# Performer block and expert block in one program on one Trainium2 core: another order of the batch loop, key sums without added constants

## The chip, the cores and the metric

One Trainium2 core runs the whole program in one launch. The metric is the device time of one execution in microseconds (us), lower is better. The time given for a kernel is the median of its runs. Engines: PE (TensorE; PEld is its weight load), DVE (VectorE), ACT (ScalarE), POOL (GpSimd), SP (SyncE, which issues most DMAs).

## The reference, cut to what matters

All tensors are float32. The input is 8 batches of 512 tokens of 256 values.

```python
# attention half, once per batch b (16 heads of 16 values, 64 random features)
a  = layernorm(x)                                 # no gain
q, k, v = a@Wq.T+bq, a@Wk.T+bk, a@Wv.T+bv         # split into heads
xp = einsum('bhnd,md->bhnm', t*16**-.25, proj)    # features of q and of k
qp = exp(xp_q - diag_q - max over m   ) + 1e-4
kp = exp(xp_k - diag_k - max over n, m) + 1e-4
out = (qp @ (kp.T @ v)) / (qp @ sum_n kp)         # heads
r  = a + out@Wo.T + bo
x2 = layernorm(r)*g2+be2
z  = layernorm(x2 + relu(x2@W1.T+b1)@W2.T+b2)*g3+be3
x1 = x + layernorm(z)
# expert half, over all 4096 tokens
xf = layernorm(x1); scores = softmax(xf@gate.T); each of 8 experts takes its top 512 tokens,
adds its two-layer MLP of them, weighted by the score; result = x1 + layernorm(that)
```

## The kernel before, in words

**Layout.** 128 partitions; a batch is TT = 4 tiles of 128 tokens. The 8 pairs of heads (PAIRS) make the 1024 columns of the key features `kp` ([128, 4, 1024]) and query features. The four PSUM banks `pX` hold features, `pA` (2 banks) the attention products, `pF` (2 banks) the feed-forward products, each used in turn: a product waits until the copy of the one before it in its bank is done.

**Stages.** A prologue, a software-pipelined loop over the 8 batches (until about 466 us), a tail that ends batch 7, the choice of the experts' tokens (about 510 to 566 us), eight experts, the last layer norm. Only the loop, the batch 0 ahead of it and SP's outputs are touched here.

**The batch loop.** `batches` calls `body(i, f, u)` on every engine: attention of batch i, feed-forward of batch f = i-1, gates and outputs of batch u = i-2, for i = 0 to 7. Bodies 3 to 6 are one hardware loop; 0, 1, 2 and 7 stand by themselves (`is_first`, `is_ahead`, `is_last`). There is no planner: each engine works off its own list in the order in which the code stands, and waits on semaphores. So the order of calls in the four `body` functions is the schedule.

**PE's list in one body.** Keys and queries (24 products of float32r, `by_halves`), values, turning x2, `key_features(0)`, turning the keys, `hidden(0)` to `hidden(7)` (six matmuls each, W1) with `key_features(1)`, `features` of the queries (two halves), `turn_kmax` and `spread_kmax` in between, then 32 products with W2 (`ff_out`, two instructions each) that are cut up to stand between `turn_tops`, `features_turned(0)`, `context`, `features_turned(1)`, `sums_of_keys`, `turn_context`, `all_heads`, `gates`, `turn_x`; `attention_out` (Wo, 24 matmuls) is last. `features` and `features_turned` run in tiles of 32 rows, `context`, `sums_of_keys`, `all_heads` and `gates` in tiles of 32 columns, all others on the full array.

**The key path.** `xk_copy` (ACT) takes the features out of PSUM; `k_max` (DVE) takes maxima; `turn_kmax`, `k_top` (`smax`, `sdiag`), `spread_kmax` make one stabilizer per head; `k_shift` and `k_sub` (DVE) subtract it; `exp_k` and then `eps_k` (ACT) give exp and exp + 1e-4; POOL adds the four token tiles into `ksum` (line 1055, three operations); `context` multiplies with v. In batch 0 there is no `eps_k`: an additional matmul with a constant adds it, and DVE does the sums.

**The query path.** `q_max` (DVE) takes maxima of the query features from PSUM, `parts_of_tops` splits them into two parts (line 1296 a cast, line 1298 a subtraction, both within SBUF), `turn_tops` (PE) turns them, `q_tops` (ACT) copies them, `features_turned` makes the shifted features anew, `exp_q` (ACT) their exp.

**The end of a body.** `all_heads` gives denominators, which `dens` (ACT) copies, and heads; `heads_out` (DVE) divides: a reciprocal (line 1313) and a product; the two groups of heads follow each other, with the gates' copy `turned_gates` (DVE) between them. `heads_top` (ACT) and `rest_of_heads` (DVE) split the result for `attention_out`.

**Layer norms.** `stats` (DVE), `root` and `shift` (POOL), `normed` (DVE) or `z_norm`, `x_norm`, `xf_norm` (ACT). `z_affine`, the two operations on x2, and `xnb` (line 1049) are POOL operations of a whole batch. `residual` (DVE, line 1336) adds x and z, both in SBUF.

Of the kernel before, what the change touches and what calls it, by code (L numbers as in the profile page):

```python
# [6 lines left out]
ALU = mybir.AluOpType  # L7
# [23 lines left out]
N_CONST = 11  # L31
# [83 lines left out]
def build(nc, video, WqT, bq, WkT, bk, WvT, bv, WoT, bo, projT, W1T, b1, W2T, b2, g2, be2, g3, be3,  # L115
          gateT, ln_w, ln_b, fc1T, b1s, fc2T, b2s, out):
    with ExitStack() as ctx:
# [39 lines left out]
        epsk_c = sb("epsk_c", [P, 1])  # L157
        eps4_c = sb("eps4_c", [P, 1])
# [3 lines left out]
        ksum = sq[:].rearrange("p a b d -> p (a b d)")  # L162
        dgk = sb("dgk", [P, TT, H])
# [14 lines left out]
        sdiag = sb("sdiag", [H, H])  # L178
        ones_h = sb("ones_h", [H, P])
        kbias = sb("kbias", [P, TT, H])  # L180
        kp = sb("kp", [P, TT, H * M])
# [13 lines left out]
        vsum = cs[:].rearrange("p n x -> p (n x)")  # L195
# [26 lines left out]
        kp_f, qe_f, qp_f = (a[:].rearrange("p a b -> p (a b)") for a in (kp, qe, qp))  # L222
# [110 lines left out]
        ksum_ready, ks_ready, ke_ready, kp_ready = sem("ksum_ready"), sem("ks_ready"), sem("ke_ready"), sem("kp_ready")  # L333
# [112 lines left out]
        def _(sp):  # L446
# [11 lines left out]
            def outputs(u):  # L458

                wait(sp, x1_out, 16 * u)  # L460
                wait(sp, xf_ready, u)
                sp.dma_start(x1[:], vid_d[u]).then_inc(xres_in, 16)

                for ready, done, dst, src in ((x1_ready, x1_out, out_t[u], x1[:]), (xf_ready, xf_out, acc_t[u], xf[:]),
                                              (y_ready, y_out, row_t[u][:, :, 0:D], y[:]),
                                              (sc_ready, sc_out, row_t[u][:, :, D:ROW], sct[:])):
                    sp.wait_ge(ready, u + 1)
                    sp.dma_start(dst, src).then_inc(done, 16)

# [35 lines left out]
            load_expert(0)  # L505
            for ready, done, dst, src in ((x1_ready, x1_out, out_t[L1], x1_end[:]), (sc_ready, sc_out, row_t[L1][:, :, D:ROW], sct[:]),
# [29 lines left out]
        def _(act):  # L536
# [40 lines left out]
            def xk_copy(i, t):  # L577

                act.wait_ge(x_ready, i * X_JOBS + J_XK + t // 2 + 1)
                nc.scalar.activation(kp[:, t, :].rearrange("p (a b) -> p a b", a=4), features_of(t), ACT.Copy).then_inc(xk_ready, 1)  # L580
# [14 lines left out]
            def cs_copy(i, n):  # L595
                act.wait_ge(a_ready, i * A_JOBS + J_CTX + n + 1)
                nc.scalar.activation(cs[:, n, :], pA[n][:, 0:G * P], ACT.Copy).then_inc(cs_ready, 1)

            def exp_k(i, t):

                act.wait_ge(ks_ready, i * TT + t + 1)
                nc.scalar.activation(kp[:, t, :], kp[:, t, :], ACT.Exp).then_inc(kp_ready if is_first(i) else ke_ready, 1)

            def eps_k(i, t):
                act.wait_ge(ke_ready, (i - 1) * TT + t + 1)
                nc.scalar.activation(kp[:, t, :], kp[:, t, :], ACT.Identity, bias=epsk_c[:, 0:1]).then_inc(kp_ready, 1)  # L606
# [91 lines left out]
            def body(i, f, u):  # L698
# [17 lines left out]
                elif att:  # L716
                    keys(i)
                    queries(i, 0)
                    queries(i, 1)
                    values(i, 0)  # L720
                    values(i, 1)
                if ff:
                    for c in range(C):
                        take_f(f, J_X2T + c, x2T_hi[:, c, :], ACT.Copy, x2T_ready)
                if is_ahead(i):
                    key_rows(1)
                elif att:
                    key_rows(0)
                    squares(i, 0)
                    squares(i, 1)  # L730
                if ff:
                    relu(f, 0)
                    relu(f, 1)
                if att and not is_ahead(i):
                    key_rows(1)
                if ff:
                    relu(f, 2)
                    relu(f, 3)
                if att:
                    q_squares(i)  # L740
                if ff:
                    for n in range(4, FC):
                        relu(f, n)
                        if ut and n < FC - 1:
                            z_norm(u, n - 4)
                        if ut and n == FC - 2:
                            z_norm(u, 3)
                if att:
                    for t in range(2):
                        exp_k(i, t)  # L750
                        eps_k(i, t)
                    q_tops(i)
                    for t in range(2, TT):
                        exp_k(i, t)
                        eps_k(i, t)
                    exp_q(i, 0)
                    cs_copy(i, 0)
                    exp_q(i, 1)
                    cs_copy(i, 1)
                if ut:  # L760
                    xf_norm(u)
                if att:
                    dens(i)
# [9 lines left out]
                if att:  # L773
                    x_norm(i + 1)
                if ut:
                    normed_rows(u)
                if att:
                    heads_top(i, 0)
                    heads_top(i, 1)
                    xT_copy(i + 1)  # L780
                if ut:
                    exp_logits(u)

# [132 lines left out]
        def _(pool):  # L916
# [8 lines left out]
            nc.gpsimd.memset(epsk_c[:], EPS_K).then_inc(const_ready, 1)  # L925
            nc.gpsimd.memset(eps4_c[:], N // P * EPS_K).then_inc(const_ready, 1)
            nc.gpsimd.memset(mxp, 0.0).then_inc(const_ready, 1)
            nc.gpsimd.memset(ones_h[:], 1.0).then_inc(const_ready, 1)

# [83 lines left out]
            def body(i, f, u):  # L1013
# [10 lines left out]
                if f is not None:  # L1024

                    pool.wait_ge(f_ready, f * F_JOBS + J_X2T + 2)
                    nc.gpsimd.tensor_tensor(x2[:], x2[:], g2_b[:].unsqueeze(1).to_broadcast([P, TT, D]), ALU.mult).then_inc(x2b_ready, 1)
                if u is not None:
                    root(3, u)
                    shift(3, u, nz)  # L1030
                if f is not None:
                    pool.wait_ge(x2b_ready, 2 * f + 1)
                    nc.gpsimd.tensor_tensor(x2[:], x2[:], b2_b[:].unsqueeze(1).to_broadcast([P, TT, D]), ALU.add).then_inc(x2b_ready, 1)
                if is_first(i):
                    root(0, 1)
                    shift(0, 1, nx)

                    pool.wait_ge(v_ready, 2)
                    halves = v.rearrange("p (k a) d -> p k (a d)", k=2)
                    nc.gpsimd.tensor_tensor(vsum[:], halves[:, 0], halves[:, 1], ALU.add).then_inc(vsum_ready, 1)  # L1040
                    pool.wait_ge(vsum_ready, 1)
                    nc.gpsimd.tensor_tensor(vsum[:, 0:D], vsum[:, 0:D], vsum[:, D:2 * D], ALU.add).then_inc(vsum_ready, 1)
                if i is not None:

                    if isinstance(i, int) and i == 0:
                        pool.wait_ge(bias_ready, 1)
# [4 lines left out]
                    for t in range(1, 1 if is_first(i) else TT):  # L1051
# [3 lines left out]
                        nc.gpsimd.tensor_tensor(ksum, kp[:, 0, :] if t == 1 else ksum, kp[:, t, :], ALU.add).then_inc(ksum_ready, 1)  # L1055
# [141 lines left out]
        def _(dve):  # L1197
# [36 lines left out]
            def k_max(i, t):  # L1234

                dve.wait_ge(xk_ready, i * TT + t + 1)
                nc.vector.tensor_reduce(mxk[:, t, :], kp[:, t, :].rearrange("p (h m) -> p h m", m=M), AX_X,
# [15 lines left out]
            def k_top(i, steps):  # L1253
# [3 lines left out]
                nc.vector.tensor_scalar(sdiag[:], ident[0:H, 0:H], smax[:, 0:1], None, ALU.mult).then_inc(stab_ready, 1)  # L1257
# [1438 lines left out]
```

## Time and profile before

| | us |
|---|---|
| median of 3 runs (787.88 to 789.0) | 787.96 |
| the profiled execution's own time | 789.41 |
| its span (first to last instruction) | 787.7 |
| PE busy, share of the span | 724.5, 92% |
| PEld busy | 592.8, 75% |
| DVE busy | 619.9, 79% |
| ACT busy | 469.8, 60% |
| POOL busy | 377.1, 48% |

Busy times are sums over the span. PE's matmuls overlap in the pipeline and their ends are modelled, so the start of one and the start of the next tell what it costs. The mean granted PE clock was 0.967 of full speed. The loop's part is the stretch to 466 us.

### The profile page before, as it was taken

What the parts mean: (1) busy time and instruction counts of PE and PEld (TensorE: products, weight loads), DVE (VectorE), ACT (ScalarE), POOL (GpSimd) and SP (SyncE); (2) the same over time, 40 slices, a digit from 0 to 9 for tenths busy, and PEclk for the clock granted to TensorE, in tenths of its full rate; (3) what the DMA queues carried; (4) which work ended last, traced back from release to release, by engine and by line L of the source; (5) the groups of instructions that cost most, each with busy time, mean ns of one, the idle gap of its engine ahead of it and who ended that gap; (6) DMA issues with size and microseconds to landing.
All of it is one profiled execution on the core that took longest, in us unless ns stands there. A gap on an engine that the chain in (4) does not pass through costs nothing. (4 is left out here: it accounts for less than half of the span.)

```text
span 787.7 us, 16101 instructions
## 1 busy us (share of the span) xinstructions
PE 724.5 (92%) x5948; PEld 592.8 (75%) x5948; DVE 619.9 (79%) x1307; ACT 469.8 (60%) x749; POOL 377.1 (48%) x358
## 2 busy tenths in 40 slices
PE   8999999999999999999999979875899999999950
PEld 7867768778778778778678668765788889998850
DVE  5876678888888888888898797888857777677683
ACT  4656747867867767868857835464245544455470
POOL 4364317527527527617616613511437576554563
PEclk9899999999999999999999999999699999999985
DMA  8100010011011011011011021250346664456593
GB/s 250 34 2 2 1 54 2 27 54 57 28 53 54 27 53 54 27 53 54 27 54 30 32 71 35 62 190 1 93 161 170 154 158 105 115 152 167 130 270 115
DMA packets 51184, 62.60 MB, mean 79 GB/s; under 512 B 9408, under 2 KB 44992, under 8 KB 51136
## 3 DMA queue, kind: packets, MB, share of 16 engines
q1 hardware_dynamic: 44016, 49.74, 19.5%
q0 software_dynamic: 6864, 12.19, 7.9%
q8 instruction: 30, 0.49, 0.3%
q14 instruction: 18, 0.15, 0.1%
q10 hardware_dynamic: 256, 0.03, 0.0%
HBM read 40.85 MB, written 21.10 MB: 79 GB/s over the span
## 5 line engine op out<-in xcount | busy, mean ns | idle before, releaser
L2166 PE MATMUL pF<-w,h 128*128 128x256 f32 x448 | 109.8, 386 | 0.0
L2166 PEld LDWEIGHTS pF<-w,h 128*128 128x128 f32 x448 | 80.7, 190 | 17.6 <-issue 8.6
L1131 POOL DMA_INDIRECT kp<-row_scratch,idx_g x32 | 43.2, 1350 | 73.5 <-DVE idx_g L1838 49.7
L896 ACT ACTIVATE h<-pX,b1cur 128x512 f32<-128x512 f32 x64 | 44.0, 689 | 53.8 <-DVE b1cur L1938 39.4
L2618 PE MATMUL pX<-w_lo,h_hi 128*128 128x256 f32 x256 | 73.9, 289 | 0.8 <-issue 0.8
L985 POOL TENSOR_SCALAR ve<-mv 128x4 f32<-128x4 f32 x36 | 8.5, 236 | 134.4 <-DVE mv L1208 133.4
L2618 PE MATMUL pX<-w_hi,h_lo 128*128 128x256 f32 x256 | 72.4, 283 | 0.0
L2618 PE MATMUL pX<-w_hi,h_hi 128*128 128x256 f32 x256 | 72.4, 283 | 0.0
L1139 POOL DMA_INDIRECT acc_scratch<-qp,idx_s x28 | 58.0, 2073 | 22.3 <-DVE qp L1875 17.4
L1896 DVE TENSOR_TENSOR h_lo<-h,h_hi 128x512 fp32r<-128x512 f32 x64 | 42.7, 690 | 24.6 <-ACT h_hi L888 24.6
L1313 DVE RECIPROCAL den<-den 128x512 f32<-128x512 f32 x14 | 46.9, 3348 | 7.9 <-ACT den L544 7.9
L1055 POOL TENSOR_TENSOR sq<-kp 128x1024 f32<-128x1024 f32 x7 | 23.3, 3333 | 61.7 <-ACT kp L606 61.7
L549 ACT ACTIVATE h<-pF,b1c 128x512 f32<-128x512 f32 x56 | 38.7, 691 | 20.6 <-PE pF L2103 20.6
L2103 PE MATMUL pX<-x2T_hi,w_lo 128*128 128x512 f32 x128 | 50.7, 396 | 0.0
L2103 PE MATMUL pX<-x2T_lo,w_hi 128*128 128x512 f32 x128 | 50.6, 395 | 0.0
L2103 PE MATMUL pX<-x2T_hi,w_hi 128*128 128x512 f32 x128 | 50.6, 395 | 0.0
L2618 PEld LDWEIGHTS pX<-w_lo,h_hi 128*128 128x128 f32 x256 | 49.0, 191 | 1.8 <-issue 1.0
L2618 PEld LDWEIGHTS pX<-w_hi,h_lo 128*128 128x128 f32 x256 | 49.0, 191 | 0.1
L2618 PEld LDWEIGHTS pX<-w_hi,h_hi 128*128 128x128 f32 x256 | 49.0, 191 | 0.0
L2103 PE MATMUL pF<-x2T_hi,w_lo 128*128 128x512 f32 x112 | 47.6, 425 | 0.5 <-DVE x2T_lo L1440 0.5
L2103 PE MATMUL pF<-x2T_hi,w_hi 128*128 128x512 f32 x112 | 44.3, 396 | 0.0
L2103 PE MATMUL pF<-x2T_lo,w_hi 128*128 128x512 f32 x112 | 44.2, 395 | 0.0
(434 smaller groups left out, 2157.9 us busy)
## 6 DMA issues: line engine op xcount, KB each, us to landing
kp<-fc1T SPq DMA_DIRECT2D x8, 1024.0 KB, 7.2
w<-fc2T SPq DMA_DIRECT2D x8, 1024.0 KB, 8.2
xin<-video SPq DMA_DIRECT2D x7, 512.0 KB, 3.7
x<-video SPq DMA_DIRECT2D x7, 512.0 KB, 4.4
out<-x SPq DMA_DIRECT2D x7, 512.0 KB, 3.0
acc_scratch<-xf SPq DMA_DIRECT2D x7, 512.0 KB, 2.9
row_scratch<-y SPq DMA_DIRECT2D x7, 512.0 KB, 3.0
kp<-acc_scratch SPq DMA_DIRECT2D x4, 512.0 KB, 5.3
```

The costliest lines, as they stand in the source:

```text
L549: nc.scalar.activation(dst, pF[n % 2][:], func, **kw).then_inc(done, 1)
L896: nc.scalar.activation(h[:, n, :], pM[n % M_SLOTS], ACT.Gelu_apprx_tanh, bias=b1cur[:, n:n + 1]).then_inc(he_ready, 1)
L985: nc.gpsimd.tensor_scalar(ve[k][:], mv[k][:, :, 1], LN_EPS, None, ALU.add).then_inc(ve_ready[k], 1)
L1055: nc.gpsimd.tensor_tensor(ksum, kp[:, 0, :] if t == 1 else ksum, kp[:, t, :], ALU.add).then_inc(ksum_ready, 1)
L1131: pool.indirect_dma_start(xg[:, g, :], None, row_d, bass.IndirectOffsetOnAxis(ap=idx_g[:, g:g + 1], axis=0)).then_inc(gathered, 16)
L1139: pool.indirect_dma_start(acc_d, bass.IndirectOffsetOnAxis(ap=idx_s[:, g:g + 1], axis=0), og[:, g, :], None, compute_op=ALU.add).then_inc( ...
L1313: steps.link(nc.vector.reciprocal(den[:, g, :], den[:, g, :]))
L1896: nc.vector.tensor_tensor(h_lo[:, n, :], h[:, n, :], h_hi[:, n, :].bitcast(F32), ALU.subtract).then_inc(h_lo_ready, 1)
L2103: ins = nc.tensor.matmul(dst[:], w_[:, k, tok(n)], x_[:, k, :], start=(m == 0), stop=(m == len(parts) - 1))
L2166: ins = nc.tensor.matmul(pF[m][:, half * D:(half + 1) * D], h[:, k, tok(2 * m + half)], w2[:, k, :], start=(k == 0), stop=(k == FC - 1))
L2618: ins = nc.tensor.matmul(pM[2 + m][:, t2 * D:(t2 + 1) * D], h_[:, k, tok(2 * m + t2)], w_[:, k, :], start=(not last and k == 0 and j == 0) ...
```

## The change

What it does:

- **Key tiles are 130 columns wide per pair.** `kp` becomes `kpe` [128, 4, 8 pairs, 130]; columns 128 and 129 hold 1e-4 from the start. `eps_k` is gone in every batch. `context` multiplies v with 129 columns, so column 128 of its result is 1e-4 times the sum of v; `cs_copy(0)` copies that column out and adds it as a bias (one small and two larger ACT operations in place of one); `cs_copy(1)` adds 512e-4 as a bias. In batch 0 the constant matmuls of `context` and `sums_of_keys` and POOL's sums of v are gone.
- **`sdiag` and `ones_h` have 128 rows** (zeros below row 16), so `spread_kmax` runs on the full array.
- **PE:** `key_features(0)` ahead of the values, `key_features(1)` ahead of `hidden(0)`, `hidden` cut differently, `turn_tops`, `context`, `features_turned(0)` next to each other, `sums_of_keys`, `features_turned(1)`, `turn_context` next to each other; W2's 32 products cut into 8, 4, 4, 5, 3, 3, 5.
- **DVE:** z is normed before `scores`; `k_max` 0 and 1 ahead of `x2T_lo`, 2 and 3 ahead of z's second statistics; `k_top` ahead of `q_max` 0 and 1; all four `k_sub` ahead of `q_max` 2 and 3 and `parts_of_tops`; `scores` of the batch before after these; both divisions ahead of `turned_gates`.
- **ACT:** `exp_k` between the last `relu`s, `z_norm` behind `exp_k`, `cs_copy` ahead of `exp_q`, `dens` ahead of `xf_norm`, `normed_rows` last.
- **POOL:** the key sums wait for all four `k_sub` first; `xnb` goes behind all roots; x2's second operation goes ahead of the third root.
- **SP:** the DMA of the scores goes one body later.

```diff
+PW = P + 2
-        kp = sb("kp", [P, TT, H * M])
+        kpe = sb("kp", [P, TT, PAIRS, PW])
+        kp = kpe[:, :, :, 0:P]
...
-                nc.scalar.activation(cs[:, n, :], pA[n][:, 0:G * P], ACT.Copy).then_inc(cs_ready, 1)
+                if n:
+                    nc.scalar.activation(cs[:, 1, :], pA[1][:, 0:G * P], ACT.Identity, bias=epsn_c[:, 0:1]).then_inc(cs_ready, 1)
+                else:
+                    wide = pA[0][:, 0:G * PW].rearrange("p (g x) -> p g x", x=PW)
+                    nc.scalar.activation(vsum[:].unsqueeze(2), wide[:, :, P:P + 1], ACT.Copy).then_inc(vsum_ready, 1)
+                    act.wait_ge(vsum_ready, i + 1)
+                    for g in range(G):
+                        ins = nc.scalar.activation(cs[:, 0, g * P:(g + 1) * P], wide[:, g, 0:P], ACT.Identity, bias=vsum[:, g:g + 1])
+                    ins.then_inc(cs_ready, 1)
...
# POOL
+                if is_first(i):
+                    pool.wait_ge(bias_ready, 1)
+                    biased_rows()
+                else:
+                    pool.wait_ge(ks_ready, (i + 1) * TT)
+                    for t in range(1, TT):
...
+                if not is_first(i):
+                    biased_rows()
...
# DVE, after kmax
                 if u is not None:
                     dve.wait_ge(za_ready, 2 * u + 2)
                     stats(3, su, z)
+                k_top(i, sa)
+                q_max(i, 0)
+                q_max(i, 1)
+                dve.wait_ge(dg_ready, (i + 1) * 2)
+                k_shift(i)
+                k_sub(i, 0)
+                k_sub(i, 1)
+                rest_of_squares(i)
+                k_sub(i, 2)
+                k_sub(i, 3)
+                q_max(i, 2)
+                q_max(i, 3)
+                parts_of_tops(i)
+                if more:
+                    ln1_stats(i + 1)
+                if u is not None and not (isinstance(u, int) and u == 0):
+                    scores(u - 1)
...
-                    heads_out(i, 0, sa)
+                heads_out(i, 0, sa)
+                heads_out(i, 1, sa)
                 if u is not None:
                     turned_gates(u * U_JOBS + J_G)
...
# PE, from key_features(1) on
+                key_features(1)
+                pe.wait_ge(x2l_ready, (f + 1) * C)
...
+                hidden(0)
+                hidden(1)
+                pe.wait_ge(qT_ready, (i + 1) * G)
+                features(i, J_XQ, qT, 0)
+                hidden(2)
+                turn_kmax()
+                hidden(3)
+                hidden(4)
+                spread_kmax()
+                hidden(5)
+                features(i, J_XQ + 1, qT, 1)
+                hidden(6)
+                hidden(7)
+                ff_out(8)
+                turn_tops()
+                context()
+                features_turned(0)
+                ff_out(4)
+                sums_of_keys()
+                features_turned(1)
+                turn_context()
+                ff_out(4)
+                all_heads()
+                ff_out(5)
```

## Rows read from the trace of the kernel before

**Rows 1.** Windows of one loop body: busy per engine (instructions), PE clock, DMA, GB/s.
```profile
260.00:319.00 59.00, 58.93 (x530) 45.19 (x529) 50.84 (x98) 43.76 (x64) 30.10 (x28) 1.00 0.13 45
```

**Rows 2.** Timeline of PE, a loop body: start, us, engine, line, out<-in, [idle before].
```profile
258.91 4.48 PE L2166 MATMUL pF<-w,h 128*128 128x256 f32 x20
263.23 0.60 PE L2073 MATMUL pX<-ident,qe 128*128 128x128 f32 x4
...
268.11 0.70 PE L2166 MATMUL pF<-w,h 128*128 128x256 f32 x2
268.74 1.95 PE L2256 MATMUL pA<-kp,qe 128*32 128x128 f32 x64
...
275.20 1.03 PE L2166 MATMUL pF<-w,h 128*128 128x256 f32 x4
276.20 3.89 PE L2175 MATMUL pA<-qp,cdbd 128*32 128x512 f32 x32
...
285.76 1.46 PE L2166 MATMUL pF<-w,h 128*128 128x256 f32 x6
286.87 0.47 PE L2297 MATMUL pX<-wo_lo,aT_hi 128*128 128x256 f32 x1
...
290.26 0.40 PE L2103 MATMUL pA<-x2T_hi,wk_lo 128*128 128x512 f32 x1
...
295.86 0.40 PE L2093 MATMUL pA<-wv_lo,x2T_hi 128*128 128x256 f32 x2
...
299.64 1.17 PE L2114 MATMUL pX<-projbd,qp 32*128 32x128 f32 x32
300.74 1.09 PE L2073 MATMUL pA<-ident,qp 128*128 128x128 f32 x8
...
312.66 0.27 PE L2182 MATMUL pA<-ident,kmax 128*16 128x128 f32 x1
```

**Rows 3.** Timeline of DVE, the same stretch.
```profile
255.21 0.94 DVE L1257 TENSOR_SCALAR sdiag<-ident,smax 16x16 f32<-16x16 f32 x1
...
257.77 2.36 DVE L1261 TENSOR_TENSOR kp<-kp,kbias 128x1024 f32<-128x1024 f32 x2
260.04 2.35 DVE L1287 TENSOR_REDUCE mxq<-pX 128x16 f32<-128x1024 f32 x2
262.52 0.20 DVE L1296 CAST qe<-mxq 128x64 fp32r<-128x64 f32 x1
262.75 0.23 DVE L1298 TENSOR_TENSOR qe<-mxq,qe 128x64 f32<-128x64 f32 x1
...
265.17 3.38 DVE L1336 TENSOR_TENSOR x<-x,z 128x1024 f32<-128x1024 f32 x1
...
312.97 0.28 DVE L1256 TENSOR_REDUCE smax<-pA 16x1 f32<-16x128 f32 x1 [0.72 <-PE pA L2182]
313.29 0.92 DVE L1257 TENSOR_SCALAR sdiag<-ident,smax 16x16 f32<-16x16 f32 x1
```

**Rows 4.** Timeline of POOL, the same stretch.
```profile
264.13 3.34 POOL L1055 TENSOR_TENSOR sq<-kp 128x1024 f32<-128x1024 f32 x1 [8.01 <-ACT kp L606]
267.55 5.70 POOL L1055 TENSOR_TENSOR sq<-sq,kp 128x1024 f32<-128x1024 f32 x2
...
311.78 2.40 POOL L1049 TENSOR_TENSOR xnb<-xn,bo_b 128x1024 f32<-128x1024 f32 x1
```

**Rows 5.** Timeline of ACT, one addition of the constant.
```profile
260.77 1.15 ACT L606 ACTIVATE kp<-kp,epsk_c 128x1024 f32<-128x1024 f32 x1
```

**Rows 6.** Timeline of DVE in body 1, which has no batch u.
```profile
81.89 0.22 DVE L1257 TENSOR_SCALAR sdiag<-ident,smax 16x16 f32<-16x16 f32 x1
```

**Rows 7.** Timeline of PE in batch 0, in body 1 and in body 7.
```profile
44.83 0.42 PE L2272 MATMUL pA<-eps_c,ones 128*32 128x128 f32 x8
...
113.63 0.50 PE L2297 MATMUL pX<-wo_hi,aT_lo 128*128 128x256 f32 x2 [1.03 <-DVE aT_lo L1277]
...
464.61 0.47 PE L2093 MATMUL pX<-wo_lo,aT_hi 128*128 128x256 f32 x2 [1.49 <-DVE aT_lo L1549]
```

More of the change, by code:

```diff
@@ L719, in body @@
                     queries(i, 1)
+                    key_rows(0)
                     values(i, 0)
                     values(i, 1)
[L722 to L728, printed above, removed]
+                for c in range(C):
+                    take_f(f, J_X2T + c, x2T_hi[:, c, :], ACT.Copy, x2T_ready)
@@ L729, in body @@
+                if not is_ahead(i):
                     squares(i, 0)
                     squares(i, 1)
[L731 to L759, printed above, removed]
+                key_rows(1)
+                relu(f, 0)
+                relu(f, 1)
@@ new lines, in body @@
+                q_squares(i)
+                for n in range(2, 6):
+                    relu(f, n)
+                exp_k(i, 0)
+                relu(f, 6)
+                exp_k(i, 1)
+                relu(f, 7)
+                exp_k(i, 2)
+                exp_k(i, 3)
+                if ut:
+                    z_norm(u, 0)
+                    z_norm(u, 1)
+                q_tops(i)
+                if ut:
+                    z_norm(u, 2)
+                    z_norm(u, 3)
+                cs_copy(i, 0)
@@ L1036, in body, with biased_rows @@
                     shift(0, 1, nx)
[L1038 to L1046, printed above, removed]
+                def biased_rows():
                     wait(pool, r_ready, i * 2)
@@ L2157, in hidden, with ff_out @@
                     by_halves(slot_f(f, J_H + n), w1_hi, w1_lo, x2T_hi, x2T_lo, n).then_inc(f_ready, 1)
-                def ff_out(m, half, k0=0, k1=FC):
-                    if half == 0:
-                        slot_f(f, J_Y + m)
-                    for k in range(k0, k1):
+                products = [(m, half, k) for m in range(2) for half in range(2) for k in range(FC)]
+                def ff_out(count):
+                    for m, half, k in products[:count]:
+                        if half == k == 0:
+                            slot_f(f, J_Y + m)
                         if m == half == 0:
@@ L2167, in ff_out @@
                                                start=(k == 0), stop=(k == FC - 1))
-                    if half == 1 and k1 == FC:
-                        ins.then_inc(f_ready, 1)
+                        if half == 1 and k == FC - 1:
+                            ins.then_inc(f_ready, 1)
+                    del products[:count]
                 def by_heads(j, w_, g):
@@ L2422, in body @@
-                if att:
-                    features(i, J_XQ + 1, qT, 1)
-                    spread_kmax()
-                if ff:
-                    hidden(7)
-                if ff:
-                    ff_out(0, 0)
-                    ff_out(0, 1, 0, 2)
-                if att:
-                    turn_tops()
-                if ff:
-                    ff_out(0, 1, 2, FC)
-                if att:
-                    features_turned(0)
-                if ff:
-                    ff_out(1, 0, 0, 1)
@@ L2438, in body @@
-                if att:
-                    context()
-                    features_turned(1)
-                if ff:
-                    ff_out(1, 0, 1, 3)
-                if att:
-                    sums_of_keys()
-                if ff:
-                    ff_out(1, 0, 3, 4)
-                if att:
-                    turn_context()
-                    if ff:
-                        ff_out(1, 0, 4, 6)
-                if att:
-                    all_heads()
+                key_features(1)
```

211 lines of the change are left out of this document (75 added, 136 removed).

## The prediction

> **What bounds the kernel now.** I read the window table first, since the share of the whole span mixes stages. In a loop body PE is busy 58.93 of 59.00 us at the full clock, the others 50.84 (DVE), 43.76 (ACT) and 30.10 (POOL) [rows 1]. So a body lasts as long as PE's own list, and a faster engine elsewhere buys nothing unless PE waited for it. The same instruction comes again after 58.08 us (`sdiag` at 255.21 and at 313.29 [rows 3]); that is a body. Since the ends of matmuls are modelled, a busy PE can hide small losses, so the second view is PE's timeline, read from start to start [rows 2]. It shows three sorts of loss. (a) The last three products with W2 start at 285.76 and Wo's first matmul at 286.87; Wo's 24 matmuls then take until 290.26, 3.39 us. 24 float32r matmuls of 512 columns take 5.60 (290.26 to 295.86), so 256 columns should take about 2.8. The W2 piece took 1.11 where six instructions at 4.32/20 = 0.216 need 1.30, so 0.19 of the 3.39 is its. The rest, 0.4 us, is a wait for the divided heads. (b) A piece of W2 between tiled work costs more than its instructions: two from 268.11 to 268.74 take 0.63 for 0.43, four from 275.20 to 276.20 take 1.00 for 0.86. That is about 0.1 at each change between the full array and tiles. (c) In bodies 1 and 7 the wait for the heads is open: 1.03, and 1.49 [rows 7].
>
> Third, DVE and POOL in the same stretch, because the new order puts DVE's query maxima under POOL's key sums [rows 3, 4]. DVE's residual of 1024 columns takes 3.38 where `k_sub` of 1024 columns takes 2.36/2. It ended at 268.55, 1.1 after POOL's first sum (264.13 + 3.34 = 267.47); POOL's next two then took 5.70 for what is otherwise 2.35 each, 1.0 more. Likewise `sdiag`, 16 columns, takes 0.92 under POOL's `xnb` (311.78 + 2.40 = 314.18, `sdiag` ends at 314.21), and 0.22 where POOL is idle [rows 6]. So these DVE operations and POOL's exclude each other.
>
> **The change part by part, a loop body.**
>
> *Work removed from ACT.* Four operations of 1.15 [rows 5], 4.6 us, against about 1 us for the cut-up `cs_copy`. ACT had 15 us of slack [rows 1] and PE did not wait for it. Taken as 0; the bounds are -0.4 (if the earlier exp took away a wait) and +0.3. PE's 129th column is 1/128 of the 1.9 us of `context` (268.74), 0.02. `spread_kmax` on the full array changes its surroundings by 0.1 at most, either way: 0.
>
> *Fewer changes of tiling.* Before, the stretch from `turn_tops` to `all_heads` changes between full array and tiles six times; after, `context` stands next to `features_turned(0)` and `sums_of_keys` next to `features_turned(1)`: four. Of the pieces of W2 inside, one is gone and two longer ones remain. At 0.1 a change and 0.1 for what the pieces lost besides: -0.3. Bounds: 0, if going from row tiles to column tiles costs as much as going by way of the full array, and -0.6, if each of the removed four sides was worth 0.15. Beyond that stretch the number of changes is the same.
> The Trainium skill ("TensorEngine Tiling (Array Packing)", Key Properties) says that changing the mode drains the engine, and row tiles and column tiles are two modes. By it the stretch has six changes instead of seven (six and `context` to `features_turned(1)`; now four and two), the term would be -0.1, and the total 1 us less good; my rows have no undisturbed step between the two kinds to test it.
>
> *The wait ahead of Wo.* Between the first of `all_heads` (276.20) and Wo stand 10 products of W2 before and 16 after (5+3+3+5), 6 x 0.43 = 2.6 us more cover for the divisions; and the second division no longer stands behind the gates' copy. The 0.4 goes: -0.4. What is late next is whatever must be ready 2.6 + 0.3 us earlier: the key and query path ahead of `all_heads`.
>
> *That path.* I walked it from `turn_kmax` to `turn_tops`. PE after: five `hidden` of 1.40 (5.60/4) = 7.0, one half of the features 1.10 (299.64 to 300.74), 8 products of 0.43 = 3.46, and `spread_kmax` with its surroundings about 0.5: `turn_tops` is wanted 12.1 after `turn_kmax`. DVE after: `turn_kmax` to `sdiag` 313.29 - 312.66 = 0.63, `sdiag` 0.22 (`xnb` no longer runs then), `q_max` 2.3, `k_shift` 0.3, `k_sub` 2.27 (257.77 to 260.04), the squares' rest 1.2 (of the size of a `k_sub`), `k_sub` 2.27, `q_max` and its gap 2.48 (260.04 to 262.52), cast and subtraction 0.46: 12.1. So the tops arrive just as PE wants them, with no margin: 0 taken, +0.7 if `sdiag` is still held up, and more in the rival below. POOL's sums start after the last `k_sub`, at about 9.2 in the same count, and end 3 x 2.43 later at 16.5; PE wants them after `turn_tops` 0.4, `context` 1.9, `features_turned(0)` (at least the 1.1 of a half of the features) and four products 1.7, at 17.2 or later. They are in time. SP's score DMA and `scores`, one body later, stand ahead of nothing that PE waits for.
>
> *Sum of a body:* -0.3 - 0.4 + 0.1 for small misfits = -0.6, five bodies (2 to 6): -3.0.
>
> **The other bodies.** Batch 0: 16 constant matmuls go (8 instructions are 0.22 to 0.42 [rows 7]), in a stretch that runs as a chain; `cs_copy(0)` gets 0.5 longer beside it. -0.7, bounds -1.0 and +0.5. Body 1: -0.3 for tiling, the wait of 1.03 and the rest of its kind, together -1.4, go; but both `k_max` now stand ahead of `x2T_lo`, where one did, and PE's `hidden(0)` waits for that: +1.2 (half of `q_max`'s 2.35, the same size); and +0.3 for tops without margin. -0.2. Body 7: its end is the chain of DVE's half divisions from `all_heads` to Wo's second half [rows 7], so it moves by the whole amount by which `all_heads` moves: 2.6 + 0.3 = -2.9. Behind it the tail is a chain, too, and nothing takes that back.
>
> Total: -3.0 - 0.7 - 0.2 - 2.9 = -6.8 us on an execution of 789.4 (span 787.7, 1.7 around it). The median of 3 is 1.45 below that execution; I carry the difference over: 787.96 - 6.8 = **781.2**.
>
> **Rivals.**
>
> *1. The subtraction of the tops waits for POOL's second sum (slower).* POOL's first sum now starts with the end of the last `k_sub`, lasts 2.36 and is followed 0.08 later by the second (267.47, 267.55 [rows 4]): that asks for the ports 2.5 after `k_sub`'s end. `q_max` starts 0.09 before that end (260.13, 260.04), the subtraction (line 1298) 2.71 after `q_max`: at 2.6. Behind POOL by 0.1, it waits for the whole second sum and PE's `turn_tops` with it: 2.4 us a body, against a gain of 0.6. It decides at 0.1 us; a POOL operation of 8 x 130 columns or one more wait ahead of it may well be that much slower, and the free-standing bodies have smaller gaps on DVE than the loop. In the four bodies of the hardware loop alone: -6.8 + 4 x 2.4 = +2.8, **790.8**. In all seven: +10, **798**.
> The Trainium skill ("SBUF — State Buffer", Who interferes with whom) states this rule: a VectorE instruction with two SBUF inputs and a GpSimd instruction that reads SBUF exclude each other for the whole instruction, and the first to issue wins. By that rule, the cast ahead of it may also take both ports. The trace agrees for the residual (3.38 for 1.2) and for `sdiag`.
>
> *2. `sdiag` is still held up,* now by the third root, which POOL starts at about the same time. For: it starts right after z's statistics, which now stand ahead of `k_top`. Against: a root works on 4 columns. Price 0.7 in each of six bodies: -6.8 + 4.2 = -2.6, **785.4**.
>
> *3. The order gains nothing in the loop:* tiling changes cost the same in any neighbourhood, a wait of 0.4 appears at another hand-over (`all_heads` for the second exp of the queries, or `turn_x`, both within 0.3 us by the same walk), and body 7 keeps a part. About -1, **787**.
>
> **How the numbers follow.** Forecast 0.46, its own range 779.0 to 784.0. Rival 1 in the loop alone 0.20, in all bodies 0.12; rival 2 0.12; rival 3 0.10. The range of 8 in 10 leaves out rival 1 in all bodies and a little below: 779.0 to 791.5. What a measurement can tell from no change is 0.2%, 1.6 us. Faster: forecast and rival 2, 0.58. Same: rival 3, 0.10. Slower: 0.32.
>
> **What would show it.** Right: `sdiag` at 0.22 us; PE's body 57.5; Wo from its first matmul to the next keys 2.8 to 3.0; the subtraction of the tops (line 1298 before) at 0.2; body 7's last wait for the heads still there, but 2.9 earlier. Rival 1: the subtraction at 2.2 to 2.6 us, PE idle ahead of `turn_tops` by as much, a body of 59.9. Rival 2: `sdiag` at 0.9, PE idle 0.7 ahead of `turn_tops`. The forecast is wrong in its base if PE waits by more than 0.3 anywhere else in bodies 2 to 6.

## The result, and the profile after

| | before | after |
|---|---|---|
| median of the runs, us | 787.91 (787.55 to 789.0, 5 runs) | 792.64 (788.32 to 798.94, 5 runs) |
| profiled execution / its span, us | 789.41 / 787.7 | 798.94 / 797.2 |
| busy PE, DVE, ACT, POOL, us (after) | | 726.3, 621.6, 443.1, 359.0 |

The ratio is 1.0055 (95% interval 1.003 to 1.008): a loss of 4.7 us against a forecast of -6.8. The second thing to see is the spread: 1.5 us before, 10.6 after. The profiled execution is the slowest of the five, so it shows the loss at its largest.

The quickest way to place a loss in a program that repeats is a list of starts of one instruction. I took the first matmul of `turn_tops` in each batch (PE's timeline) and subtracted:

| kernel | batch 0 to 1 | 1 to 2 | 2 to 3 | 3 to 4 | 4 to 5 | 5 to 6 | 6 to 7 | 7 to the turn of x2 | behind it |
|---|---|---|---|---|---|---|---|---|---|
| before | 52.53 | 57.29 | 57.97 | 58.07 | 58.08 | 58.07 | 58.08 | 28.73 | 321.5 |
| after | 51.62 | 55.80 | 59.50 | 62.03 | 62.09 | 59.42 | 57.50 | 29.27 | 322.0 |
| `e1_guard` (below) | 51.39 | 55.79 | 57.46 | 57.45 | 57.40 | 57.40 | 57.49 | 29.32 | 321.9 |

One thing in this table is bookkeeping: the change puts 16 matmuls with W2 ahead of the tops where 20 stood, so from body 1 on the tops come 4 x 0.23 = 0.9 us earlier within a body. That 0.9 shows as a gain in the first period and is missing again behind the tops of batch 7.

The loss sits in four bodies, 3 to 6, which are the passes of the hardware loop. There PE stands still ahead of the turned tops. PE in body 4 (timeline: start, us, engine, line, out<-in, idle before and its releaser):

```profile
263.74 1.24 PE L2159 MATMUL pF<-w,h 128*128 128x256 f32 x5
266.90 0.94 PE L2064 MATMUL pX<-ident,qe 128*128 128x128 f32 x4 [1.92 <-DVE qe L1300]
267.77 3.30 PE L2247 MATMUL pA<-kp,qe 128*32 128x129 f32 x64
271.00 1.14 PE L2202 MATMUL pX<-qT,projbd 32*128 32x512 f32 x8
...
282.23 1.92 PE L2169 MATMUL pA<-qp,cdbd 128*32 128x512 f32 x16 [0.96 <-ACT den L554]
```

The releaser is the subtraction of the tops. DVE and then POOL in the same stretch; they answer to [rows 3, 4]:

```profile
261.90 2.35 DVE L1289 TENSOR_REDUCE mxq<-pX 128x16 f32<-128x1024 f32 x2
264.38 0.20 DVE L1298 CAST qe<-mxq 128x64 fp32r<-128x64 f32 x1
264.61 2.24 DVE L1300 TENSOR_TENSOR qe<-mxq,qe 128x64 f32<-128x64 f32 x1
...
279.05 2.14 DVE L1307 TENSOR_TENSOR csum_own<-csum,epsmask 128x8 f32<-128x8 f32 x1
```
```profile
262.15 2.37 POOL L1054 TENSOR_TENSOR sq<-kp 128x1024 f32<-128x1024 f32 x1 [7.16 <-DVE kp L1263]
264.60 4.42 POOL L1054 TENSOR_TENSOR sq<-sq,kp 128x1024 f32<-128x1024 f32 x2
...
278.79 2.37 POOL L1043 TENSOR_TENSOR xnb<-xn,bo_b 128x1024 f32<-128x1024 f32 x1
```

POOL's second key sum starts at 264.60, DVE's subtraction at 264.61; the subtraction, 0.22 us of work, takes 2.24 and ends when POOL's second sum does (4.42 is the time of the second and the third together). In all four loop bodies POOL is ahead by 0.01 us or level; in bodies 1 and 2 the subtraction starts 0.06 before (89.20 and 89.26, 145.00 and 145.06) and takes 0.22. The same thing happens once more at 279.05: POOL's `xnb`, 0.26 us ahead, holds an 8-column product for 2.14; the bias that `dens` (ACT) waits for comes from that product, and the last two head products wait 0.96 for ACT's copies.

A third price comes from PE's clock (windows: us, then PE, PEld, DVE, ACT, POOL busy, granted clock, DMA, GB/s). First body 4, its stop and the 4.2 us behind it, then the same in body 5:

```profile
264.90:266.90 2.00, 0.08 (x1) 0.00 (x1) 2.00 (x2) 0.34 (x1) 1.92 (x2) 1.00 0.00 0
266.90:271.10 4.20, 4.20 (x72) 3.39 (x72) 3.76 (x15) 1.58 (x3) 2.12 (x1) 0.59 0.00 0
```
```profile
327.00:328.90 1.90, 0.06 (x1) 0.00 (x0) 1.90 (x2) 0.32 (x1) 1.85 (x1) 1.00 0.00 0
329.00:331.40 2.40, 2.40 (x68) 2.10 (x68) 2.00 (x11) 1.57 (x3) 2.12 (x1) 1.00 0.00 0
```

After 1.92 us without work the granted clock was 0.59 on average in body 4, between its levels of 1.2 and 2.4 GHz, and the turned tops with `context` took 4.10 us; after the same stop in body 5 it stayed at 1.00 and they took 2.48 (328.99 to 331.47). So a body that loses takes 2.0 more, and in two of the four 2.6 on top, 1.6 of it the clock and 1.0 the wait at 282.23.

The stop ahead of body 3's tops was followed by a slow stretch too (0.60 over 204.87 to 209.00), the one ahead of body 6's was not.

What the forecast named for the loop body itself is there. PE and DVE, bodies 5 and 6, answering to [rows 2, 3]:

```profile
353.01 0.47 PE L2285 MATMUL pX<-wo_lo,aT_hi 128*128 128x256 f32 x1
...
356.00 0.39 PE L2094 MATMUL pA<-x2T_hi,wk_lo 128*128 128x512 f32 x1
```
```profile
374.86 0.22 DVE L1258 TENSOR_SCALAR sdiag<-ident,smax 16x16 f32<-16x16 f32 x1
```

Wo takes 2.99 us instead of 3.39, `sdiag` 0.22 instead of 0.92. In the last batch, DVE's copy of the gates and PE's two waits ahead of Wo, answering to [rows 7]:

```profile
465.85 0.29 DVE L1345 COPY gT<-pF 128x128 f32<-128x128 f32 x1 [2.66 <-PE pF L2130]
```
```profile
465.13 0.65 PE L2130 MATMUL pF<-qe,gate 128*32 128x128 f32 x16
...
469.06 0.47 PE L2084 MATMUL pX<-wo_lo,aT_hi 128*128 128x256 f32 x2 [1.79 <-DVE aT_lo L1540]
...
473.60 0.48 PE L2084 MATMUL pX<-wo_lo,aT_hi 128*128 128x256 f32 x2 [0.62 <-DVE aT_lo L1540]
```

### The profile page after: what moved, and what is told of

It reads as the page before. It is cut to its first block and busy times, and to the rows that moved or that the text cites. A ratio compares the mean times of both kernels' runs of the same rounds, so it can differ in the third digit from the quotient of the medians.

```text
span 797.2 us, 16016 instructions
## 1 busy us (share of the span) xinstructions
PE 726.3 (91%) x5916; PEld 597.3 (75%) x5916; DVE 621.6 (78%) x1307; ACT 443.1 (56%) x737; POOL 359.0 (45%) x357
## 5 line engine op out<-in xcount | busy, mean ns | idle before, releaser
L2159 PE MATMUL pF<-w,h 128*128 128x256 f32 x448 | 106.5, 384 | 0.0
L1238 DVE TENSOR_REDUCE mxk<-kp 128x16 f32<-128x1024 f32 x32 | 37.5, 1213 | 6.9 <-ACT kp L590 6.9
```

The costliest lines, as they stand in the source:

```text
L1238: nc.vector.tensor_reduce(mxk[:, t, :].rearrange("p (s h) -> p s h", h=2), kp[:, t].rearrange("p s (h m) -> p s h m", m=M), AX_X, ALU.max) ...
L2159: ins = nc.tensor.matmul(pF[m][:, half * D:(half + 1) * D], h[:, k, tok(2 * m + half)], w2[:, k, :], start=(k == 0), stop=(k == FC - 1))
```

## The experiments

Each was timed in 4 to 12 runs against runs of the kernel before on the same chip. The main theory: in the loop the subtraction of the tops and POOL's second key sum are in a dead heat, and a lost one costs a body 2 us or more. The rivals: the new order of PE's work or the 129th column costs the time; the spread is only the granted clock's. Different experiments ran on different chips, so a comparison between two of them rests on the ratios to the kernel before, or on the traces.

**`e1_guard`.** POOL's second sum also waits for the tops' two parts.

```
                         if t > 1:
                             pool.wait_ge(ksum_ready, i * (TT - 1) + t - 1)
+                        if t == 2:
+                            pool.wait_ge(qmx_ready, (i + 1) * TOPS)
```

> The changed kernel, and POOL's second key sum also waits until the tops' two parts are stored. Theory (a dead heat between the subtraction of the tops and that sum): the subtraction takes 0.22 us in all 8 batches, PE goes from W2 to the turned tops without a wait, and the five runs lie within 1.5 us of one another. From the changed kernel's profiled 798.9 go 4 stalls of 1.93 and 1.8 of slow PE behind one of them: about 789.4, so 787 to 790. Rival (the loss is in the new order of PE's work, or in the 129th column): 791 to 794, as the changed kernel. Rival (the spread is the granted clock's own): the runs still spread over 5 us or more.

Measured: 784.56 us (784.39 to 785.75), ratio 0.9947 (0.9932 to 0.9963). The subtraction takes 0.22 in all 8 batches and the row of the table above has no body over 57.5. DVE, then POOL, in body 4:

```profile
259.06 0.23 DVE L1302 TENSOR_TENSOR qe<-mxq,qe 128x64 f32<-128x64 f32 x1
```
```profile
259.36 4.50 POOL L1056 TENSOR_TENSOR sq<-sq,kp 128x1024 f32<-128x1024 f32 x2 [0.39 <-DVE qe L1302]
```

The time is 2.4 us below the expected range, which had counted four stops and one slow stretch, and neither the second slow stretch nor the waits at the head products. The first rival falls: the same PE order with the same 129 columns is now 4.2 us faster than before. The spread goes from 10.6 us to 1.4, but a spread alone proves no race: the kernel before, on another chip, came to 786.62 to 792.83 us at granted clocks of 0.971 to 0.958. What speaks against the clock as the only cause is two runs of the changed kernel at the same granted clock, 0.967, that took 788.32 and 792.64. The 14.4 us between the two profiled spans are almost all in four periods: 2.0 + 4.6 + 4.7 + 2.0 = 13.3.

**`e2_late` and `e8_lost`.** Can the race be made always lost?

```
                 nc.vector.tensor_copy(hi.bitcast(F32R), whole).then_inc(qmx_ready, 1)
+                nc.vector.memset(spare[:], 0.0)
```

> The changed kernel, and a memset of 64 columns on DVE between the cast and the subtraction of the tops, so that POOL's second key sum is always first. Dead heat theory: the subtraction takes 2.0 to 2.2 us in each of the 7 bodies instead of in some, PE waits some 2 us ahead of the turned tops in each, and the time is the guarded kernel's plus 7 x 2.0 = 14 us or a little more (803 to 806), with a small spread between runs. If the subtraction's start has nothing to do with it, the extra 0.1 us a body gives 793 to 794.

Measured: 787.7 us; five of the six runs lie between 783.66 and 793.58, one at 795.43. Neither expectation holds, and the edit was weaker than meant: the name belonged to a scratch of one column. DVE and POOL in the profiled execution:

```profile
258.19 0.20 DVE L1299 CAST qe<-mxq 128x64 fp32r<-128x64 f32 x1
258.33 0.06 DVE L1300 MEMSET spare<- 128x1 f32 x1
258.41 0.23 DVE L1302 TENSOR_TENSOR qe<-mxq,qe 128x64 f32<-128x64 f32 x1
```
```profile
258.41 4.54 POOL L1055 TENSOR_TENSOR sq<-sq,kp 128x1024 f32<-128x1024 f32 x2
```

The 0.06 us fell into the gap behind the cast, so the subtraction started 0.22 after the cast, as without it. In bodies 3 to 6 POOL's sum started 0.01 ahead of it or level, just as in the changed kernel's profiled execution, and yet DVE won all four here and lost all four there: starts that are equal to 0.01 us don't tell who wins. Another run of the same kernel on the same chip came to 793.58 at the granted clock of this one (0.967 and 0.966), 10 us apart. I take the difference for lost races; only the fast execution was profiled, so this isn't shown. With 512 columns (0.48 us) the edit does what was meant:

> The changed kernel, and a memset of 512 columns (0.2 us or more) on DVE between the cast and the subtraction of the tops. With the memset of 0.06 us POOL and DVE still started within 0.01 us of each other and DVE won each time. Theory (the one that is ready first by more than that holds the other out): the subtraction is held for 1.9 to 2.2 us in bodies 1 to 7, each body is 59.4 to 62.1 long instead of 57.4, and the time is 798 to 806 with a spread of a few us from the granted clock. Rival (not the order but something else decides, and a later subtraction shares the port): 785 to 788.

Measured: 795.83 us (793.41 to 802.06), ratio 1.0094 (1.0057 to 1.013); periods 59.46, 62.04, 62.03, 59.45 in the loop. PE and the windows behind two of the stops:

```profile
268.32 0.91 PE L2066 MATMUL pX<-ident,qe 128*128 128x128 f32 x4 [1.92 <-DVE qe L1302]
283.64 1.92 PE L2171 MATMUL pA<-qp,cdbd 128*32 128x512 f32 x16 [0.94 <-ACT den L555]
```
```profile
268.40:270.40 2.00, 2.00 (x28) 1.58 (x32) 1.81 (x10) 1.14 (x3) 2.00 (x1) 0.55 0.00 0
...
330.40:332.40 2.00, 2.00 (x59) 1.83 (x63) 1.82 (x10) 1.36 (x3) 2.00 (x1) 1.00 0.00 0
```

The theory holds for the loop and its price; it was wrong that bodies 1, 2 and 7 would lose too, and the median lies below the expected 798 to 806. In 1 and 2 the memset started 0.04 to 0.05 ahead of POOL's sum, in the loop 0.03 to 0.04 behind it; in 7 POOL waits 0.44 of its own. In those three bodies the subtraction took 0.15 us although POOL's sum had started 0.36, 0.36 and 0.07 before it, and POOL's pair of sums took up to 4.89 instead of 4.54. So it seems that the memset kept POOL out until the subtraction had started; no run isolates that. The runs still spread over 8.6 us: where the profiled execution lost all four, the price of a lost race is 2.0 or 4.6, so a spread doesn't count the races either.

**`e10_nudge`.** The opposite push: POOL 0.3 later, no wait added.

```
                         if t > 1:
                             pool.wait_ge(ksum_ready, i * (TT - 1) + t - 1)
+                        if t == 2:
+                            settled(pool)
+                            nc.gpsimd.tensor_scalar(nudge_c[:], mhalf[:], LN_EPS, None, ALU.add)
```

(`settled` is one semaphore increment, no wait.)

> The changed kernel, and POOL does one operation of 4 columns (0.2 us) between its first and second key sum; no wait is added. Theory (whoever is ready first holds the other out, and a few hundredths of a us decide): POOL's second sum comes 0.3 us later, DVE's subtraction takes 0.22 in all bodies, 784 to 786 with a spread under 2.5 us. Rival (only an order kept by a wait cures it, since the two engines' times vary between runs): 786 to 794, spread over 4 us.

Measured: 783.02 us (781.29 to 784.17), ratio 0.993 (0.9915 to 0.9946), a little below what was expected, the spread 2.9 instead of under 2.5. DVE and POOL in body 4:

```profile
258.00 0.20 DVE L1302 CAST qe<-mxq 128x64 fp32r<-128x64 f32 x1
258.23 0.23 DVE L1304 TENSOR_TENSOR qe<-mxq,qe 128x64 f32<-128x64 f32 x1
```
```profile
258.34 0.23 POOL L1057 TENSOR_SCALAR nudge_c<-mhalf 128x4 f32<-128x4 f32 x1 [0.20 <-POOL sq L1058]
258.53 4.51 POOL L1058 TENSOR_TENSOR sq<-sq,kp 128x1024 f32<-128x1024 f32 x2
```

0.3 us of distance are as good as a wait: the periods from 2 to 7 are 57.33 to 57.43.

**`e11_cover`.** Is the price PE's standstill, or something behind it on DVE or POOL? (`e8_lost`, with `ff_out(12)`, `ff_out(2)`, `ff_out(2)` in place of 8, 4, 4.)

> The kernel in which POOL is always first in the loop (memset of 512 columns), and 4 of the 8 W2 products that lie behind the turned tops (in two groups) are moved ahead of them: 0.93 us of work while PE waits. Theory (the price of the lost race is PE's idle time, and the granted clock falls after it): PE's idle ahead of the tops goes from 1.92 to about 1.0, some of it comes back as waits of 0.2 to 0.6 further on, and a body in which the clock stays up takes 58.8 to 59.4; where the clock does not fall any more the 2.6 us bodies go too: 790 to 796. Rival (the price lies in DVE's or POOL's later work, not PE's idle): as without this edit, 795 to 796.

Measured: 793.12 us (792.39 to 794.96), ratio 1.0071 (1.0055 to 1.0087). A product is two matmuls of 0.23, so I had counted half: 1.86 us of work moved. PE in body 4:

```profile
264.50 0.66 PE L2066 MATMUL pX<-ident,qe 128*128 128x128 f32 x4 [0.21 <-DVE qe L1302]
270.79 1.14 PE L2204 MATMUL pX<-qT,projbd 32*128 32x512 f32 x8 [0.33 <-ACT qp L639]
274.61 3.80 PE L2171 MATMUL pA<-qp,cdbd 128*32 128x512 f32 x32 [0.53 <-ACT qp L639]
```

The subtraction is still held (1.82), but PE idles 0.21, the clock stays at 1.00 (read behind the tops of bodies 3, 4 and 5), and no body takes 62: the four of the loop take 58.7 each. `csum_own` is not held either (0.17). So the 4.6 us bodies were PE's standstill and what it drew after it. It is no cure: the work that now covers the tops is missing behind them, at two waits for the queries' exp.

**`e3_xnb`.** The guard, and POOL's bias sum behind DVE's reduction (`pool.wait_ge(obias_ready, i + 1)` ahead of `biased_rows()`).

> The guarded kernel, and POOL adds the bias to the normed rows only once DVE has reduced the context's sums. Theory: the product of 8 columns ahead of that reduction takes 0.17 us in all batches instead of up to 2.1, PE's wait ahead of the four head products (1.0 in two bodies, a part of 1 in the last) goes: 1.5 to 2 us less than the guarded kernel, 786 to 788. Rival (ACT's norm of the next rows waits for the later bias sum, or the held product was covered): within 0.5 us of the guarded kernel.

Measured: 786.58 us (784.48 to 787.03), 2.0 above `e1_guard`. `csum_own` takes 0.17 everywhere, and the loop bodies take 57.41: the rival holds. There was nothing to gain in the bodies, since with the guard alone the product took 0.17 in them already; it was held in batch 0 (0.97) and batch 7 (1.43) only. The 2.0 lie elsewhere: 0.98 in the first period, 1.5 behind batch 7, in code that is the same. The granted clock was 0.964 in five of its six runs, 0.967 to 0.969 in those of `e1_guard`, and its one run at 0.967 took 784.48, as `e1_guard` does. I take it for the clock's; the next run, which keeps the edit, bears this out.

**`e4_tail`.** The last one, and in the last batch the copy one place later.

```
             end_heads(1, 0)
-            turned_gates((L2 - 1) * U_JOBS + J_G)
             end_heads(0, 1)
+            turned_gates((L2 - 1) * U_JOBS + J_G)
             end_rest_of_heads(0)
```

> The kernel before this one, and in the last batch DVE copies the gates behind the fourth half head instead of ahead of it. Theory: the copy waited 2.66 us for gates that PE issues 16 matmuls later than it did, and Wo waited 1.79 and 0.62 behind it: 2.0 to 2.4 us less, 784 to 786. Rival (the chain of four half divisions sets the end of that batch whatever the copy does): within 0.5 us of the kernel without this edit.

Measured: 781.89 us (781.01 to 784.27). From the tops to the turn of x2 27.01 us instead of 29.18: -2.2, as expected. The median fell by 4.7, 2.5 more than the edit explains, to below the expected 784 to 786: the first period is back at 51.41 us and the stretch behind the turn takes 320.5 instead of 323.3, the granted clock in its first 7.3 us 1.00 instead of 0.78. That is what `e3_xnb` had lost, and POOL's wait is still in place. DVE and PE, against the rows of the last batch above:

```profile
451.52 0.29 DVE L1348 COPY gT<-pF 128x128 f32<-128x128 f32 x1 [0.48 <-PE pF L2133]
```
```profile
452.59 0.58 PE L2087 MATMUL pX<-wo_lo,aT_hi 128*128 128x256 f32 x2
...
457.09 0.47 PE L2087 MATMUL pX<-wo_lo,aT_hi 128*128 128x256 f32 x2 [0.48 <-DVE aT_lo L1543]
```

**`e7_gates_mid`.** On `e4_tail`, the copy between the two divisions again, in the bodies.

> The kernel with guard, bias sum and tail edits, but DVE copies the gates between the two divisions again, as before the change; PE's gates stay where the change put them. Theory (the tail's loss is a copy that waits for gates issued later): the second division starts at the end of PE's gates, some 2.8 us later in every body, and Wo or the stage behind it waits 1 to 2.5 us of that: 5 to 14 us more in all. Rival (there is slack on DVE behind the divisions): within 0.5 us.

Measured: 783.93 us (782.5 to 784.84) on one chip, `e4_tail` 781.89 on another (ratios 0.9942 and 0.9917). The traces are clearer: 57.84 a body instead of 57.41. DVE and PE in body 5:

```profile
337.14 0.29 DVE L1348 COPY gT<-pF 128x128 f32<-128x128 f32 x1 [2.87 <-PE pF L2133]
```
```profile
341.36 0.47 PE L2288 MATMUL pX<-wo_lo,aT_hi 128*128 128x256 f32 x1
...
344.75 0.40 PE L2097 MATMUL pA<-x2T_hi,wk_lo 128*128 128x512 f32 x1
```

The copy waits 2.87 as expected, but only 0.4 reaches PE: Wo takes 3.39 instead of 3.00. DVE's slack hid the rest, so both expectations missed; and 3.39 is what Wo took before [rows 2]. The divisions side by side are what took that wait away.

**`e6_split`.** On `e4_tail`, W2's products between the tiled groups again.

```
                 turn_tops()
+                ff_out(3)
                 context()
                 features_turned(0)
-                ff_out(4)
+                ff_out(1)
                 sums_of_keys()
+                ff_out(1)
                 features_turned(1)
+                ff_out(1)
                 turn_context()
-                ff_out(4)
+                ff_out(2)
                 all_heads()
```

> The kernel with guard, bias sum and tail edits, but W2's products are again put between the groups that use PE in tiles (tops, 3 products, context, features, 1, key sums, 1, features, 1, turned context, 2, heads); the number of products ahead of the heads and behind them is unchanged. Theory (what a body gained by standing the tiled groups side by side is about 0.3 us): the body goes from 57.4 to 57.6 to 57.8, 1.5 to 2.8 us in all. Rival (the order of PE's groups gains nothing and the 0.65 us a body came from the copy of the gates and Wo's cover alone): within 0.5 us.

Measured: 786.35 us (784.58 to 788.38); 58.0 a body. From tops to heads it takes 11.41 us, `e4_tail` 10.83. `e6_split`, then `e4_tail`:

```profile
382.21 0.70 PE L2162 MATMUL pF<-w,h 128*128 128x256 f32 x2
382.84 0.64 PE L2262 MATMUL pA<-sq,ones 128*32 128x128 f32 x16
383.42 0.70 PE L2162 MATMUL pF<-w,h 128*128 128x256 f32 x2
384.26 1.14 PE L2205 MATMUL pX<-qT,projbd 32*128 32x512 f32 x8
```
```profile
378.43 1.99 PE L2162 MATMUL pF<-w,h 128*128 128x256 f32 x8
380.35 0.65 PE L2262 MATMUL pA<-sq,ones 128*32 128x128 f32 x16
380.92 1.14 PE L2205 MATMUL pX<-qT,projbd 32*128 32x512 f32 x8
```

Two matmuls between tiled groups take 0.63 and 0.84 for 0.46; eight take 1.92 for 1.86. Of the 0.58, two small waits belong to this order and not to the tiling: 383.42 + 0.70 leaves 0.14 ahead of the features (ACT's exp of the queries ends there), and the heads wait 0.13 for the masked context. That leaves 0.3, by subtraction. So the gain of standing the tiled groups side by side is 0.3 us in this comparison, which still mixes several changes of neighbour. The total, 3.6 us by spans (4.5 by medians from two chips), is more than I expected, since I had left those waits out.

**`e5_body1`, `e9_best`, `e12_all`.** On `e4_tail`, in body 1 only, `k_max(i, 1)` behind the low parts of x2T (`e5_body1`); that without the later bias sum (`e9_best`); and with `e10_nudge`'s operation in place of the guard (`e12_all`).

> The kernel with guard, bias sum and tail edits, and in body 1 (whose keys are ready ahead) DVE takes the second key maximum behind the low parts of x2T instead of ahead of them. Theory: PE's wait of 1.25 us ahead of the first hidden product of body 1 goes, so 0.8 to 1.2 less than the kernel without this edit. Rival (the key maxima then end later and the turn of kmax waits): 0 to +0.5.

Measured: 781.65 us (780.01 to 782.22). The period from batch 0 to 1 is 50.60 instead of 51.41, and the wait is down from 1.25 to 0.47:

```profile
69.77 0.50 PE L2100 MATMUL pF<-x2T_hi,w_lo 128*128 128x512 f32 x1 [0.47 <-DVE x2T_lo L1442]
```

> The changed kernel with guard, tail and body 1 edits, without the later bias sum. Theory (that sum lay beside the path: bodies of 57.4 us with it and without it, and the 2 us between the two medians were the granted clock's): within 0.7 us of the kernel with all four, 781 to 782.5. Rival (the bias sum's wait cost the 2 us): 779 to 780.5.

Measured: 782.39 us (780.1 to 784.21): 0.7 above `e5_body1`, which ran on another chip (ratios 0.9926 and 0.9909). The rival (the bias sum's wait costs 2 us) wanted it 1 to 2 us below, and falls.

> The kernel with later bias sum, tail and body 1 edits, and POOL's 4-column operation in place of the guard's wait. From the traces: bodies of 57.33 instead of 57.42 us (6 of them: 0.5 less), the rest as in the kernel with all four edits: 780 to 782, spread under 4 us. If the small operation loses the race in some run, that run shows 2 us or more above the others for each such body.

Measured: 779.92 us (778.34 to 780.4, 4 runs), ratio 0.9889 (0.9873 to 0.9906): 8.6 us faster than the kernel before, bodies of 57.32 to 57.42. It is the best version found.

## Why the prediction was wrong, step by step

**The step that failed** is the term for the path ahead of the tops: they come "just as PE wants them, with no margin: 0 taken". Measured, PE stands still for 1.92 us there in each of four bodies, and with what follows the four cost 13.3 us (`after` against `e1_guard`). The term rests on the weighing of rival 1, which had the mechanism, the place and the four bodies right, and got 0.20. By the forecast's own sum POOL asks 2.5 after `k_sub`'s end and the subtraction comes at 2.6; measured, they come within 0.01. A dead heat at the resolution of the rows is not a case to be given a small chance: even the best of the changed kernel's five runs, 788.3, lies above the worst of the guarded kernel's six, 785.8. The Trainium skill ("SBUF — State Buffer", Who interferes with whom) has the rule that the first to issue wins and holds the other out for the whole instruction. Where the starts are clearly apart, `e1_guard`, `e10_nudge` and the loop of `e8_lost` agree with it: 0.22 us when first, 1.8 to 2.2 when second. The forecast cited it, and its own count put POOL first; it should have been the forecast.

**Rival 1's price was too small in two bodies, and its number is near by luck.** It asked 2.4 a body for the held sum. PE's stop was 2.0, and two of the four bodies paid 2.6 more, for the clock (1.6) and for a second exclusion (`csum_own` behind `xnb`, 1.0) that only a late body meets. Its 790.8 stands near the median of 792.6 by luck: both of its terms are too low, since without any race the change gains 4.9 and not 6.8, and the four lost races of the profiled execution (798.9) cost 13.3 and not 9.6. The other runs paid less. How many races they lost isn't shown; the fastest lies 3.8 above `e1_guard`, about two at 2.0 each, an estimate from runs on two chips.

**Body 7: -2.9 forecast, -0.3 measured.** In the table the last stretch is 0.6 longer, and 0.9 of that is the shift of the tops named there. The chain of four half divisions was read off the kernel before; that the gates' copy stands inside this chain in the last batch was not counted. The change puts 16 matmuls with W2 between the heads and the gates where 4 stood, 12 more (the expectation of `e4_tail` says 16). The copy then waits for the gates 2.66 us and the chain behind it with it. `e4_tail` gives 2.2 of it back by moving the copy, and with it the term is -2.65 against -2.9.

**The loop body: -0.6 forecast, -0.64 measured** (58.08 to 57.44, mean of four periods of `e1_guard`); 2 to 6 together -3.0 forecast, -3.1 measured. Its terms: Wo's wait -0.4, measured 0.4 twice, in Wo's length and in `e7_gates_mid`. Tiling -0.3: the stretch from tops to heads took 12.98 with 24 matmuls of W2 (5.57 at 0.232 each) before and takes 10.83 with 16 (3.71), so 7.41 against 7.12: -0.29. By the rule of the Trainium skill on modes ("TensorEngine Tiling (Array Packing)", Key Properties), weighed in the prediction, it would be -0.1; the measurement is nearer to my rows, though it does not isolate a step from row tiles to column tiles. The 129th column: `context` 1.90 us instead of 1.88, as taken.

**Batch 0 and body 1: -0.9 forecast, -2.6 by the table** (`e1_guard` against before). 0.9 of it is the shift of the tops, which the forecast has in body 7, and 0.8 a slow clock in the kernel before ahead of the first features (2.48 us against 1.68; the granted clock was 0.73 from 38 to 40 us, 1.00 in `e1_guard`). That leaves the -0.9 of the forecast, though one of its terms was off: the second `k_max` was taken at +1.2 and costs 0.8 (`e5_body1`).

**Rivals 2 and 3** are out: `sdiag` takes 0.22 in all 8 batches, and the order gains 0.64 a body.

The sum for the guarded kernel against before, by spans and as the table counts: start -0.1, batch 0 and body 1 -2.6, bodies 2 to 6 -3.1, body 7 +0.6, behind it +0.3: -4.9 us. So even without the races the -6.8 was too much, mainly by body 7. The changed kernel adds 14.4 to that in its profiled execution.

Open: why, in the loop, the memset of `e8_lost` that started 0.03 behind POOL was not slowed (0.48 as elsewhere) while, in bodies 1 and 2, POOL's pair of sums behind the memset took 4.89 instead of 4.54. And why the clock fell after two of four equal stops, in both kernels after the first two.

## What to carry to other kernels

Where two engines can hold each other out, compare the two starts to a hundredth of a microsecond. Here 0.01 us went either way, while in the traces 0.06 on the right side won each time, and with 0.3 (`e10_nudge`, `e12_all`) no body was lost and the runs spread by 2.9 and 2.1 us. If your count can't separate the starts, plan with the lost race, or buy the distance: a wait or 0.2 us of idle work on the engine with slack was worth 8 to 10 us here (ratios of 0.9947 and 0.993 in place of 1.0055). A spread that grows between runs of one kernel (1.5 to 10.6 us) is a reason to look for such a race, not a proof of it, since the granted clock spreads runs too. And when a producer is moved, look at each copy of the consumer's order: the loop's had been changed with it, the last batch's had not.

## What the hardware showed that I had not expected

- An elementwise operation of 8 columns on DVE, two inputs in SBUF, took 2.14 us behind a POOL operation of 1024 columns that had started 0.26 us earlier.
- With recorded starts equal to 0.01 us, POOL won four times of four in one kernel's trace and DVE four times of four in another's (`e2_late`), two of whose runs on one chip took 783.66 and 793.58 us at granted clocks of 0.966 and 0.967.
- After 1.92 us without a matmul, PE's granted clock was 0.60 and 0.58 on average over the next 4.1 us in bodies 3 and 4, and 1.00 in bodies 5 and 6, in the changed kernel and in `e8_lost` alike; after 0.21 us (`e11_cover`) it stayed at 1.00.
- One stop can cost more than its length: 4.6 us for 2.0, until the work behind it is back in step.
